# Ten of twelve modulation blocks moved from the lead-in into the first attention

## What is computed

```python
proj = t_emb @ W_ada.T + b_ada                       # layer 0
scale, shift = (proj[:, :C], proj[:, C:])
h = (x - mu) * jax.lax.rsqrt(var + LN_EPS)
h = h * (1.0 + scale[:, None, :]) + shift[:, None, :]
q = (h @ Wq.T)...; c_kv = h @ Wkd.T                  # 16 heads of 32, latent of 128
k = (c_kv @ Wku.T)...; v = (c_kv @ Wvu.T)...         # 4 key/value heads
q = q * cos + _rotate_half(q) * sin                  # rope; k the same
out = softmax(masked(q @ k.T / sqrt(32))) @ v @ Wo.T
...
scale = time_emb @ tw.T                              # layer 1, twice
ada = silu(cond) @ Wada.T + bada                     # layer 2, six parts
eo = silu(emb) @ emb_W + emb_b                       # layer 3, two parts
```

## Time and profile before

| | |
|---|---|
| median of 3 runs | 2400.38 us (2399.41 to 2405.69) |
| the profiled execution's own time | 2398.59 us |
| its span | 2396.8 us, 34593 instructions |
| PE busy | 2244.7 us (94%) |
| ACT, DVE, POOL busy | 1033.6, 1168.9, 292.5 us |
| first scores of batch 0 / of batch 1 (start) | 93.49 / 181.98 us |
| chain that ended last | PE 84%, ACT 7%, DVE 6% |

### The profile page before, as it was taken

One profiled execution on the slowest core, in us unless ns is written; L12 is line 12 of the kernel. 1 busy time (PEld: TensorE's weight loads), 2 busy tenths in 40 slices (PEclk: granted clock), 3 DMA queues, 4 the chain that ended last, 5 costly groups with the idle time before them and its releaser, 6 DMA issues.

```text
span 2396.8 us, 34593 instructions
## 1 busy us (share of the span) xinstructions
PE 2244.7 (94%) x14034; PEld 1511.1 (63%) x14034; DVE 1168.9 (49%) x2499; ACT 1033.6 (43%) x2425; POOL 292.5 (12%) x246
## 2 busy tenths in 40 slices
PE   5889999999999999999999989999999989999998
PEld 2455555555555687888877756565664668888633
DVE  2345454454457344433443356657587554544322
ACT  2355555444446221111113366657676552222473
POOL 3331122122021001110001010101010110000021
PEclk9889999999999999999999999999999999999999
DMA  8310020000010002110102211011110101100001
GB/s 274 113 40 27 15 64 26 23 23 18 18 40 27 31 27 84 54 61 27 36 6 79 79 53 67 31 63 36 54 36 19 53 1 36 36 1 1 1 18 53
DMA packets 59487, 104.97 MB, mean 44 GB/s; under 512 B 10592, under 2 KB 24560, under 8 KB 59328
## 3 DMA queue, kind: packets, MB, share of 16 engines
q1 hardware_dynamic: 58368, 100.30, 12.6%
q0 software_dynamic: 960, 2.45, 0.3%
HBM read 77.04 MB, written 10.49 MB: 37 GB/s over the span
## 4 chain that ended last, share of the span: by engine, by line
PE 84%; ACT 7%; DVE 6%; POOL 1%; issue 1%; SPq 1%; DMA 1%; DVEq 0%; POOLq 0%; ACTq 0%
PE banks L1213 36%; PE banks L404 22%; PE banks L740 6%; PE banks L732 4%; PE banks L756 4%; ACT sb_Pr L842 2%; PE banks L766 2%; PE banks L265 1%; ACT sb_PT L847 1%; PE banks L906 1%; DVE sb_hN L364 1%; PE banks L630 1%; PE banks L638 1%; DVE sb_Pr L812 1%; PE banks L890 1%
## 5 line engine op out<-in xcount | busy, mean ns | idle before, releaser
L1213 PE MATMUL banks<-sb_HH,sb_Ws 128*128 128x512 f32 x1536 | 490.2, 392 | 12.7 <-DVE sb_HL L1103 7.3
L1213 PEld LDWEIGHTS banks<-sb_HH,sb_Ws 128*128 128x128 f32 x1536 | 289.6, 189 | 76.7 <-issue 16.7
L1213 PE MATMUL banks<-sb_hidH,sb_Ws 128*128 128x512 f32 x1024 | 331.2, 392 | 0.4 <-DVE sb_x L1284 0.4
L842 ACT ACTIVATE sb_Pr<-sb_Pr,sb_nmax 128x512 f32<-128x512 f32 (+4 forms) x512 | 291.6, 576 | 30.9 <-DVE sb_nmax L812 30.8
L1213 PE MATMUL banks<-sb_HL,sb_Ws 128*128 128x512 f32 x768 | 300.0, 391 | 0.0
L847 ACT ACTIVATE sb_PT<-banks 128x512 f32<-128x512 f32 (+2 forms) x320 | 143.5, 496 | 302.6 <-PE banks L740 225.5
L740 PEld LDWEIGHTS banks<-sb_ident,sb_Pr 128*128 128x128 f32 x1536 | 169.7, 142 | 125.5 <-issue 38.9
L819 DVE COPY sb_PT<-banks 128x512 f32<-128x512 f32 (+2 forms) x320 | 168.6, 563 | 163.1 <-PE banks L740 108.7
L740 PE MATMUL banks<-sb_ident,sb_Pr 128*128 128x128 f32 x1536 | 214.2, 282 | 18.2 <-DVE sb_A L830 5.0
L1213 PEld LDWEIGHTS banks<-sb_hidH,sb_Ws 128*128 128x128 f32 x1024 | 192.3, 188 | 44.0 <-issue 2.5
L1213 PE MATMUL banks<-sb_hidL,sb_Ws 128*128 128x512 f32 x512 | 199.4, 389 | 0.0
(11 more groups left out here) (160 smaller groups left out, 3251.7 us busy)
## 6 DMA issues: line engine op xcount, KB each, us to landing
sb_ring<-split_units SPq DMA_DIRECT2D x48, 512.0 KB, 3.3
sb_ropet<-sb_R SPq DMA_DIRECT2D x70, 128.0 KB, 2.0
sb_staged<-in_L_cond_Wfc SPq DMA_DIRECT2D x16, 512.0 KB, 4.6
sb_wada<-in_L_cond_Wada SPq DMA_DIRECT2D x6, 1024.0 KB, 5.5
split_units<-sb_unitpair SPq DMA_DIRECT2D x12, 512.0 KB, 2.9
sb_x<-in_x SPq DMA_DIRECT2D x4, 1024.0 KB, 9.1
sb_staged<-in_L_cond_Wg SPq DMA_DIRECT2D x8, 512.0 KB, 3.7
sb_staged<-in_L_cond_Wu SPq DMA_DIRECT2D x8, 512.0 KB, 4.7
```

What stands on the lines that cost most here:

```text
L842: ins = e.activation(prob, prob if s.biased else k.bank(n % 4)[:, 0:s.width(u)], ACT.Exp, bias=s.stat(k, k.nmax, b, u), scale=-1.0 if s.bi ...
L1213: mm = e.matmul(bank, lhsT, rhs, start=i == 0, stop=i == len(mats) - 1)
```

## The change

Only blocks 0 and 1 remain in the lead-in, woven among `norm0`, and batch 0's x is loaded ahead of them. The angles' reduce moves behind `norm0`, sine and cosine behind the first rope tile. `lead` lists k's rope (`r0[0]`) after the second group of q, where it stood after all of `proj0`. Blocks 2 to 11, the last turn and the combinations are put among `norm0` and `proj0` of batch 1, in attention 0; behind these come, one after the other, the whole rope of batch 1 and `norm0` of batch 2, which were interleaved. Weights get four buffers: 0 and 1 lie in what batch 1's q and k use later, 2 in that of `wo1`, 3 in batch 1's attention output. SP loads blocks 4 to 11 behind the 15 copies of batch 0's k, each when block n - 2 is done, and layer 1's weights when turn 11 is done. Layer 0's weights, `perm`, cosines and sines move from POOL's queue to SP's. Nothing in the computation is left out.

```diff
-        wada = [place(f"wada{i}", 30464 + 2048 * i, [P, C, D]) for i in range(3)]
+        wada = [place(f"wada{i}", o, [P, C, D]) for i, o in enumerate((17408, 19456, 6144, 23552))]
...
+        wada_of = lambda j: j if j < 2 else 2 + j % 2
...
-                return scores_end(*p) if p else []
+                return scores_end(*p) if p else [("ada", 0, "block", 1)] if b else []
...
-                return [("post" + p[0][-1], p[1], "mm", C - 1)] if p else []
+                return [("post" + p[0][-1], p[1], "mm", C - 1)] if p else [("ada", 0, "block", BLOCKS - 1)] if b else []
...
-        start = pre(0, 0, 1, 2)
         blocks = [ada.block(0), ada.block(1) + ada.turn(0), ada.turn(1)] + \
             [ada.block(j) + (ada.turn(j - 1) if j > 2 else []) for j in range(2, BLOCKS)] + [ada.turn(BLOCKS - 1)]
-        lead = [(ada, 0, "act", "silu", 0), (angles, 0, "dve", "reduce", 0), (angles, 0, "act", "sin", 0),
-                (angles, 0, "act", "cos", 0), (angles, 0, "dve", "negate", 0)] + start[0] + sum(blocks[:3], []) + \
-            fold(start[1:], (0, len(start) - 1, blocks[3:])) + [(ada, 0, "act", "scales", 0)] + \
-            [(ada, 0, "dve", "comb", i) for i in range(len(combs))]
+        n0, p0, r0 = pre(0, 0), pre(0, 1), pre(0, 2)
+        turned = [(angles, 0, "act", "sin", 0), (angles, 0, "act", "cos", 0), (angles, 0, "dve", "negate", 0)]
+        lead = [(ada, 0, "act", "silu", 0)] + \
+            sum([n0[0], blocks[0], n0[2], blocks[1], n0[3], blocks[2], n0[5], n0[6], [(angles, 0, "dve", "reduce", 0)],
+                 p0[0], p0[1], p0[6], p0[2], r0[0], turned, p0[3], r0[1], p0[4], r0[2], p0[5], r0[3], p0[7], r0[4]], [])
+        combs_after = [(ada, 0, "act", "scales", 0)] + [(ada, 0, "dve", "comb", i) for i in range(len(combs))]
...
-            sides01.append(([] if m else pre(1, 0)) + pre(m + 1, 1) + among(late, pre(m + 1, 2), pre(m + 2, 0)) + [[]])
+            if m == 0:
+                sides01.append(among(pre(1, 0) + pre(1, 1), blocks[3:] + [combs_after]) + pre(1, 2) + pre(2, 0) + [[]])
+            else:
+                sides01.append(pre(m + 1, 1) + among(late, pre(m + 1, 2), pre(m + 2, 0)) + [[]])
...
+            load_x(0)
+            load_block(0)
+            load_block(1)
+            for dst, name in ((wkd, "L0_cond_Wkd"), (wq0, "L0_cond_Wq")):
+                e.dma_start(dst, rows(name)).then_inc(l_w[0], 16)
...
+            load_x(1)
+            load_block(2)
...
+            load_x(2)
+            load_x(3)
+            done("angles", 0, "cos", 0)
+            load_block(3)
+            e.dma_start(wo0, rows("L0_cond_Wo")).then_inc(l_wo0, 16)
...
+                if b == 0:
+                    for n in range(4, len(blocks)):
+                        done("ada", 0, "block", n - 2)
+                        load_block(n)
+                    done("ada", 0, "turn", len(blocks) - 1)
+                    for dst, name in ((wk1, "L1_cond_Wk"), (wv1, "L1_cond_Wv"), (wo1, "L1_cond_Wo")):
+                        e.dma_start(dst, rows(name)).then_inc(l_w[1], 16)
```

More of the change, by code:

```diff
@@ L1848, in _, with load_x @@
             xrows = a["x"].rearrange("(c p) b t -> p c b t", p=P)
[L1849 to L1864 removed]
+            def load_x(b):
+                e.dma_start(x[:, :, b, :], xrows[:, :, b, :]).then_inc(l_x[b], 16)
```

67 lines of the change are left out of this document (29 added, 38 removed).

## The result

The change makes the kernel slower: a median of 2421.60 us (2412.23 to 2425.16, six runs) against 2399.89 us (2399.13 to 2405.69, six runs), a ratio of 1.0081, 95% interval 1.0061 to 1.0101. Run once more beside other kernels it came to 2420.30 against 2401.61. I had forecast 2404, within 2390 to 2417.

What follows compares the result with a forecast made beforehand. PE was taken as full almost everywhere, with room only at the beginning. Lead-in -36.6 and attention 0 +40.2 gave net +3.6: 2402.2 us from the profiled execution, 2404 from the median; own range 2396 to 2412, overall 2390 to 2417.

Steps and rivals of the forecast that it cites:

- Lead-in: From the start to the first scores: x first and k's rope forward with blocks out, together -36.6 us.
- x first: Lead-in: batch 0's x loaded early, so projections start near 27 us instead of 44.1, -17 (between -14 and -19).
- my own mark of 60: Sign at the end of the lead-in: a start of scores above 60 us makes the lead-in forecast wrong.
- The work: Attention 0: ten blocks and ten turns at 1.0 us each in PE's full list, +20 us.
- the hand-over: Attention 0: turns wait for ACT's copy of the block out of shared bank 7, +7 us (5 to 12).
- the late places: Attention 0: ACT or DVE late through a second exponentials' table load and blocks behind norm0's squares and shifts, +5 (1 to 8).
- the clock: Start of attention 0: PE comes to quad 0 with about 2 us of waiting, not 6.76; -4.5 us (0 to -6).
- Rival A: Attention 0: hand-over waits keep PE at half clock up to quad 6 or further, +16, 2420 us; chance 0.13.
- The rope: Attention 0, quad 11: batch 1's k is ready later, its sine product standing behind quad 11's maxima, +3.3 us.
- Late next: After tile 2's swap lands: rope tiles, then batch 2's sums, mean, variance and scales stand behind it, +9.4 us (5 to 12).
- Rival C: Attention 0: the moved blocks fill existing waits, net -10.8, 2389.6 us; chance 0.17.
- above 196: Sign: PE through batch 2's scale after 196 us means A; near 188 was forecast, below 180 means C.

Runs made afterwards that it cites:

- a_split: Changed kernel with each block and each turn a place of its own in the first attention's list; 2413.73 us against 2402.03 for the kernel before.
- a_again: The changed kernel, unedited, run once more for a second profile; 2420.30 us against 2401.61 for the kernel before.
- c_fill_swaps: c_lead_swaps plus one unused 128x512 product behind each of blocks 7 to 11 and the last turn; 2375.04 us against 2401.61 for the kernel before.
- c_lead: Changed kernel with the ten blocks back in the lead-in, four weight buffers, x first and k's rope forward kept; 2389.02 us against 2402.03 before.
- c_lead_swaps: c_lead with swaps of rope tiles 2 to 4 ahead of the copies of k from batch 1 on; 2382.88 us against 2402.03 before.
- a_warm: Changed kernel with four unused 128x512 products at the end of the lead-in; 2422.86 us against 2402.03 for the kernel before.
- a_fill: Changed kernel with one overwritten 128x512 product ahead of each of the ten moved blocks; 2425.99 us against 2402.10 for the kernel before.
- a_inter: Changed kernel with batch 1's ropes and batch 2's norm again in turns in the first attention; 2411.05 us against 2402.03 for the kernel before.
- a_all: Changed kernel with swaps ahead of k's copies, ropes and norm in turns, blocks and turns in own places; 2395.56 us against 2401.61 before.

## Why the prediction was wrong

The working against both profiles of the changed kernel, by its own steps:

| step | forecast | first profile | second |
|---|---|---|---|
| projections start | 27 | 26.98 | 27.65 |
| scores start | 56.8 | 59.13 | 59.03 |
| quad 0 to quad 11 | 85.9 | 90.5 | 96.6 |
| quad 11 to k ready | 3.3 | 5.5 | 5.7 |
| k ready to tile 2's sine | 13.9 | 13.85 | 13.86 |
| from there until PE is through the scale of batch 2 | 28.3 | 30.9 | 31.1 |
| to the layer-1 tables | 427.7 | 426.3 | 430.0 |

(85.9 is the 58.4 of before plus 20, 7 and 5 less 4.5. "Through the scale" is the start of the transposes that the prediction dates with 184.75 in the kernel before; in the two profiles they start at 199.88 and 206.26. 427.7 is 612.48 less 184.75.)

**Lead-in: right.** x first gave 17.1 us of the 17. The scores were 2.3 us later than forecast: I had costed block 3 and `wo0` ahead of the copies at nothing, with 1 to 3 us if the cover went. k was ready at 44.0, but SP issued the copies only from 45.56 (`wo0`'s issue alone took 1.60), and their issues took 12.04 us instead of 10.78. By my own mark of 60 the lead-in stands.

**The work, the hand-over, the late places: right in kind.** The first attention has the waits at L139 that I named, 0.72 at the least, 8.6 us in nine of them in the first profile and 10.1 in the second, against a range of 5 to 12. (The ten waits of 9.6 us in the expectation of a_split count one of the lead-in.) a_split gains 7.0 us by halving them, the size of the term. The table load took its 1.28.

**The step that failed is the clock.** I gave it -4.5, on the ground that PE would come to quad 0 with only 2 us of waiting and keep full clock. In its place the clock was at half in the slices behind quad 0 and fell again before quad 11 (in the first profile 0.65 and 0.50 from 56 to 72 us, 0.57 and 0.58 from 88 to 104). The blocks and turns took 26.3 us in the first profile instead of 20 (14.1 and 12.2), and everything between them was drawn out too. Against the forecast, quad 11 is 4.6 us late on that stretch in the first profile and 10.7 in the second: with the other terms as forecast, the clock cost about 0 and 6 us there where I had it give 4.5. The median is some 9 us above the first profile; a_again puts such a run beside it, and the two differ in the clock and in little else that I can find.

Two things were wrong in the step. Its ground, that the 6.76 us of waiting before quad 0 had brought the clock down in the kernel before, does not explain it: in c_fill_swaps PE has full clock up to 80 us and comes to quad 0 without a wait, and the clock falls in the first quads all the same. What a start at full clock is worth can be read there too: 57.8 us from quad 0 to quad 11, against 58.4 in c_lead and 59.6 in c_lead_swaps, so 0.6 to 1.7 us and not 4.5. And the step had nothing for what the moved work itself does to the clock.

**Rival A** had this result and its price (+16, 2420) within 2 us of the median. I gave it 0.13. Its condition was even met (4.47 us idle before quad 0). But that condition is not the cause: in a_warm, without that wait, the clock falls just the same, in the slice from 64 to 72 us. Its reason, the waits at each hand-over, is not borne out either: a_split halves them and its clock is no higher, and in c_lead the clock falls with no wait at all. What the fall follows, by c_lead, c_fill_swaps and a_fill, is the kind of work: where blocks and turns stand without full products between them it drops, although PE is busy. That is shown for the lead-in; in the first attention, where the first quads lower the clock too, how much of it the blocks do is not measured apart.

The page that spoke for A says that half rate is the default which activity lifts (the Trainium skill, TensorE: Matmul & The Clock Gate, The HAM clock gate). This case's traces agree in that no idle time is needed for the clock to fall; but PE was busy for 8.00 of 8.00 us in c_lead's slice from 72 to 80 and the clock was at 0.50, so being busy was not enough there. I had read idle time only.

**The rope:** quad 11 to k ready was 2.2 us more than forecast. The maxima end 2.1 us after quad 11's first score, since DVE has batch 1's near values (`VN`) to copy first; two sines stand together (2.36 us); and POOL's two steps beside them took 1.78 and 1.53 instead of 1.27. **Late next:** a_inter prices it at 9.7 against 9.4. The row itself is 2.6 us over the forecast: from the start of the mean to that of the variance it took 11.3 us instead of 7.9, with quads 14 and 15 between them at half clock. The forecast's own terms add up to less than it says: a mean that starts at T + 12.7, 7.9 to the variance and 1.9 for it give T + 22.5, not T + 24, so by them the row would have been 26.8. The wait before quad 13 (forecast about 10, from 150 to 160) was 13.8 for these reasons.

**Rival C** needed attention 0 to swallow the blocks; a_all against c_lead_swaps shows that even with its waits repaired it does not.

The signs given: projections at 27 and scores below 60 came true; the turns' waits, 0.72 to 2.19, mostly too; batch 2's scale through "above 196" was the sign for A, and it was 200.

## What to carry to other kernels

Side work that is moved from idle time into a full stretch costs its own time, its hand-overs, and what it does to the clock; read the last from a place where this kind of work runs alone, not from how busy PE will be. Before moving work out of a lead-in, see whether the lead-in's own order is the fault: here x first and k's rope forward, with the blocks behind it, won 13 us with nothing moved into the attention (no run tells the two apart). And where one queue carries transfers with different due times (swaps wanted at once, copies of k wanted some 20 us later), put them in order of need: that was worth some 10 us in both kernels by the medians and stood in the earlier trace rows before any change.

## What I had not expected of the hardware

- Matmuls that are useless can make a kernel faster: six full products more, 3.1 us less by the traces and 7.5 by the medians (c_fill_swaps). TensorE fell from 2.4 to 1.2 GHz while it was busy without a gap (c_lead, near 69 us), and with full products between it did not.
- The same program spreads by 13 us over six runs (2412 to 2425), and within it the time goes with the mean clock (0.974 to 0.968). That side work makes the time less certain is not shown, though: five more runs of it spread by 5.1 us, and the kernel before by 6.6 over six runs and 9.7 over seventeen.
- A single DMA issue on SP took 2.87 and 3.28 us (`wq0` and `wku`, at 4.37 and 7.28 us in the first profile), with 3.25 MB and more issued on the queue just before, and the next one, of `wvu`, 0.43 us.
- A table load between DVE's maxima and ACT's exponentials took 1.28 us, and the next activation started 0.02 us after it (60.25 to 61.55). ACT had been idle before it; but the load at 41.04 came 0.02 us after the end of an activation and the next one followed 0.02 us after it (42.34), so no drain was to be seen on either side.
